# Softmax reciprocals spread by two small DMAs through DRAM, one bias tile per graph, and the waits in another order

## The reference, cut to what matters

```
h = max(layernorm(x), 0); x = x + cheb(h, adj)           # Chebyshev propagation, 4 orders
h = max(layernorm(x), 0); x = x + attention_net(h, adj)  # tanh encoder, 2 masked attention layers, 3-layer MLP
h = max(layernorm(x), 0); x = x + relu(norm_adj @ (h @ W))
h = max(layernorm(x), 0); t = adj @ h; x = x + where(t > 0.5, t / t, 0)

def att_layer(h, mask):                                  # inside attention_net, twice per graph
    v, q, k = tanh(h @ wv + bv), tanh(h @ wq + bq), tanh(h @ wk + bk)
    att = softmax(q @ k.T * mask - 9e15 * (1 - mask), axis=2)
    return att @ v
```

## Time and profile before

| | |
|---|---|
| median of 3 runs | 888.2 us (886.36 to 890.27) |
| profiled execution, its own time | 887.01 us |
| its span (first to last instruction) | 885.2 us |
| PE busy | 768.6 us, 87% of the span |
| DVE busy | 576.3 us, 65% |
| ACT busy | 445.8 us, 50% |
| POOL busy | 388.1 us, 44% |
| DMA | 22.77 MB, 26 GB/s over the span |

### The profile page before, as it was taken

How to read it: one execution, slowest core, us unless ns; L and a number is a source line. 1 busy time by engine, 2 the same in 40 slices (tenths; PEclk the granted TensorE clock), 3 DMA queues, 4 the chain that set the end, 5 groups by cost and what they waited for, 6 DMA issues and landing times.

```text
span 885.2 us, 11494 instructions
## 1 busy us (share of the span) xinstructions
PE 768.6 (87%) x3776; PEld 541.5 (61%) x3808; DVE 576.3 (65%) x1631; ACT 445.8 (50%) x929; POOL 388.1 (44%) x491
## 2 busy tenths in 40 slices
PE   2658799999989899999989999998989999998774
PEld 2435566666766666666766666675766666675543
DVE  3266668577677767677677767667676767765432
ACT  2035645637364654737464553736464563735330
POOL 3134534555353535555353435546263445543301
PEclk9969999999999999999999999999999999999996
DMA  6100100102010100201010100102010010000000
GB/s 168 39 1 0 54 1 5 56 1 59 1 60 1 57 4 0 60 1 60 1 61 1 30 31 0 60 1 61 1 60 0 14 47 1 7 1 7 1 7 6
DMA packets 29276, 22.77 MB, mean 26 GB/s; under 512 B 19488, under 2 KB 21024, under 8 KB 29216
## 3 DMA queue, kind: packets, MB, share of 16 engines
q1 hardware_dynamic: 29216, 22.03, 8.3%
HBM read 19.93 MB, written 2.10 MB: 25 GB/s over the span
## 4 chain that ended last, share of the span: by engine, by line
PE 38%; DVE 22%; POOL 18%; issue 17%; ACT 4%; POOLq 0%; DVEq 0%
PE turn_ps L1056 7%; PE pre_ps L936 5%; PE post_ps L936 4%; POOL rstd_pre L414 4%; DVE u L831 3%; PE turn_ps L1039 3%; POOL rstd_post L414 3%; POOL k_lo L486 2%; DVE h_nat_pre L706 2%; PE pre_ps L899 2%; PE pre_ps L953 2%; POOL centred_pre L417 2%; POOL centred_post L417 2%; DVE score_ps L795 2%; DVE negz L803 2%
## 5 line engine op out<-in xcount | busy, mean ns | idle before, releaser
L589 ACT ACTIVATE negz<-negz,negmax 128x512 f32<-128x512 f32 x128 | 92.3, 721 | 72.0 <-DVE negmax L803 72.0
L414 POOL TENSOR_TENSOR rstd_post<-vareps_post,nhalf 128x4 f32<-128x4 f32 x32 | 32.8, 1026 | 210.1 <-DVE vareps_post L691 210.1
L1056 PE MATMUL turn_ps<-pt,v_n 128*128 128x512 f32 x256 | 115.2, 592 | 0.0
L803 DVE CUSTOM_DVE_ANT_0 negz<-score_ps,gate 128x512 f32<-128x512 f32 x128 | 88.5, 692 | 19.7 <-DVE score_ps L795 6.2
L795 DVE TENSOR_TENSOR score_ps<-score_ps,a_nat 128x512 f32<-128x512 f32 x128 | 89.1, 696 | 17.1 <-PE score_ps L1025 16.1
L936 PE MATMUL pre_ps<-at_hi,u_pair_pre 128*128 128x512 f32 x192 | 87.6, 456 | 7.3 <-DVE u_pair_pre L728 5.2
L414 POOL TENSOR_TENSOR rstd_pre<-vareps_pre,nhalf 128x4 f32<-128x4 f32 x32 | 34.0, 1061 | 131.1 <-DVE vareps_pre L691 131.1
L548 ACT ACTIVATE y_t_pre<-pre_ps 128x512 f32<-128x512 f32 x48 | 28.7, 597 | 123.3 <-PE pre_ps L936 123.3
L596 ACT ACTIVATE pt<-turn_ps 128x512 f32<-128x512 f32 x128 | 74.0, 593 | 15.8 <-PE turn_ps L1039 13.9
L936 PE MATMUL post_ps<-at_hi,u_pair_post 128*128 128x512 f32 x128 | 55.7, 435 | 29.5 <-DVE u_pair_post L728 29.5
L1039 PEld LDWEIGHTS turn_ps<-ident,negz 128*128 128x128 f32 x512 | 61.2, 141 | 32.3 <-issue 16.1
(11 more groups left out here) (137 smaller groups left out, 1815.4 us busy)
## 6 DMA issues: line engine op xcount, KB each, us to landing
a_nat<-in_adj SPq DMA_DIRECT2D x16, 1024.0 KB, 5.8
x_in<-in_x SPq DMA_DIRECT2D x16, 128.0 KB, 2.8
out<-x_out SPq DMA_DIRECT2D x16, 128.0 KB, 1.9
cheb_ws<-in_L_gnn_weight SPq DMA_DIRECT2D x2, 64.0 KB, 4.7
att_w<-in_L_gnn_a_wv SPq DMA_DIRECT2D x2, 64.0 KB, 2.4
att_w<-in_L_gnn_a_wk SPq DMA_DIRECT2D x2, 64.0 KB, 2.2
att_w<-in_L_gnn_a_wq SPq DMA_DIRECT2D x2, 64.0 KB, 2.2
bv_f<-in_L_gnn_a_bv SPq DMA_DIRECT2D x2, 64.0 KB, 2.7
```

The costliest lines, as they stand in the source:

```text
L414: gp.tensor_tensor(rstd[t][:], vareps[t][:], nhalf[:, 0:RB], ALU.pow)\
L589: sc.activation(probs[:, i, :], negz[:, i, :], ACT.Exp, bias=negmax[:, i:i + 1], scale=-1.0, accum_out=total[:, i:i + 1]).then_inc(probs_d ...
L803: ve.tensor_tensor_reduce(negz[:, i, :], score_ps[i % 2][:], gate[:, i, :], -1.0, 3.0e38, ALU.add, ALU.min, negmax[:, i:i + 1]).then_inc(b ...
L1056: mm = te.matmul(turn_ps[0][:], v_n[a][:, j * P:(j + 1) * P], pt[:, j, :], start=(j == 0), stop=(j == RB - 1))
```

## The change

Three edits go together.

1. `spread_inv` on PE and `copy_inv` on ACT are gone. In their place SP issues two DMAs for each attention layer (`spread`): the 128 x 4 reciprocals to a 2 KB tensor in DRAM, `inv_d`, and, when that has landed, from there to all 128 partitions of `inv_row`. They come from DRAM in the order partition, then block, so DVE reads `inv_row` with a step of four elements (16 bytes).
2. `gate` is made once per graph, at the place of the first attention layer.
3. Where an instruction has several waits, their order in the source is turned in nine places, so that the one that comes last in time is written first.

```diff
 "tensor":  ... keys.1-1 turn_a1-0 [spread_inv.2-2 taken out] values.1-1 turn_a2-0 turn_a3-0 attend.2-2 ...
 "scalar":  copy_inv.2-2 and copy_inv.1-1 taken out
 "gpsimd": """
-        norm_cheb-0 add_cheb_bias-0 split_qk.1-1 mask_bias.1-1 inverse_roots-0 cheb_u3-0
-        norm_gcn-2 mask_bias.2-1 split_qk.2-1 cheb_f0-0 norm_last-2 norm_enc-0
+        norm_cheb-0 add_cheb_bias-0 split_qk.1-1 mask_bias-1 inverse_roots-0 cheb_u3-0
+        norm_gcn-2 split_qk.2-1 cheb_f0-0 norm_last-2 norm_enc-0
...
+        inv_d = nc.dram_tensor("inv_d", [P, RB], F32)
...
+            def spread(g, a):
+                sp.wait_ge(inv_done, 2 * g.n + a + 1)
+                if follows(g, a):
+                    sp.wait_ge(inv_spread, 16 * (2 * g.n + a))
+                sp.dma_start(inv_d[:], inv_total[:]).then_inc(inv_sent, 16)
+                sp.wait_ge(inv_sent, 16 * (2 * g.n + a + 1))
+                if follows(g, a):
+                    sp.wait_ge(attended, 2 * g.n + a)
+                sp.dma_start(inv_row[:], inv_d.rearrange("p i -> (p i)").partition_broadcast(P))\
+                    .then_inc(inv_spread, 16)
...
-            load(Graph(0, 3))
-            store(Graph(0, 0))
-            for n in range(1, B):
+            spread(Graph(0, 0), 0)
+            for n in range(B):
+                if n:
+                    store(Graph(0, n - 1))
+                spread(Graph(0, n), 1)
                 if n + SLOTS < B:
                     load(Graph(0, n + SLOTS))
-                store(Graph(0, n))
+                if n + 1 < B:
+                    spread(Graph(0, n + 1), 0)
+            store(Graph(0, B - 1))
...
@@ mask_rows (DVE)
-                if i == 0:
-                    dve.wait_ge(gate_done, 2 * g.n + a + 1)
+                dve.wait_ge(masked, 8 * g.n + n + 1)
+                if n == 0:
+                    dve.wait_ge(gate_done, g.n + 1)
                 if follows(g, a):
                     dve.wait_ge(pt_ready, 8 * g.n + n - 3)
-                dve.wait_ge(masked, 8 * g.n + n + 1)
@@ invert (DVE)
                 dve.wait_ge(probs_done, 8 * g.n + 4 * a + 4)
+                if follows(g, a):
+                    dve.wait_ge(inv_sent, 16 * (2 * g.n + a))
@@ attend (DVE)
-                dve.wait_ge(inv_copied, 2 * g.n + a + 1)
                 dve.wait_ge(pv_ready, 2 * g.n + a + 1)
-                ve.tensor_tensor(to[:], turn_ps[0][:], inv_row[:], ALU.mult).then_inc(attended, 1)
+                dve.wait_ge(inv_spread, 16 * (2 * g.n + a + 1))
+                ve.tensor_tensor(to[:].rearrange("h (i p) -> h i p", p=P),
+                                 turn_ps[0][:].rearrange("h (i p) -> h i p", p=P),
+                                 inv_row[:].rearrange("h (p i) -> h i p", i=RB),
+                                 ALU.mult).then_inc(attended, 1)
```

More of the change, by code:

```diff
@@ L471, in cheb_f0, with mask_bias @@
                 pool_pre.add(gp.tensor_tensor(c_diff[:], c_diff[:], over_blocks(d_root[:]), ALU.mult))
+                pool.wait_ge(pool_pre.sem, pool_pre.so_far())
                 pool.wait_ge(cheb_taken, 3 * g.n + 3)
-                pool.wait_ge(pool_pre.sem, pool_pre.so_far())
                 gp.tensor_tensor(f0[:], f0[:], c_diff[:], ALU.add).then_inc(f0_done, 1)
-            def mask_bias(g, a):
-                if follows(g, a):
-                    pool.wait_ge(biased, 8 * g.n + 4 * a)
+            def mask_bias(g):
+                if follows(g):
+                    pool.wait_ge(biased, 8 * g.n)
                 gp.tensor_scalar(gate[:], a_nat[g.slot][:], -1.0, NEG, ALU.add, ALU.mult)\
@@ L507, in _ @@
                 "add_mlp_bias": add_mlp_bias,
-                **layer(0, split_qk=queries_keys, mask_bias=mask_bias),
+                "mask_bias": mask_bias,
+                **layer(0, split_qk=queries_keys),
                 **layer(1, split_qk=queries_keys),
-                **layer(1, mask_bias=mask_bias),
                 "norm_gcn": scale_norm("post", 0), "norm_last": scale_norm("post", 1),
@@ L599, in copy_pt @@
                 return f
-            def copy_inv(g, a):
-                act.wait_ge(inv_ready, 2 * g.n + a + 1)
-                sc.activation(inv_row[:], turn_ps[1][:], ACT.Copy).then_inc(inv_copied, 1)
             def mlp(k, to, ps, bias):
@@ L696, in norm_apply @@
                 dve.wait_ge(rstd_done[t], 4 * g.n + 2 * k + 2)
+                if t == "pre" and k == 0 and follows(g):
+                    dve.wait_ge(ht_ready, 2 * g.n)
                 to = h_nat[t][:, :, 0, :] if t == "pre" else h_nat[t][:]
@@ L735, in cheb_norm @@
             def cheb_norm(g):
-                if follows(g):
-                    dve.wait_ge(ht_ready, 2 * g.n)
                 norm_apply("pre", dve_pre, g, 0)
@@ L1041, in turn_rows, with attend @@
                 mm.then_inc(pt_ready, 1)
-            def spread_inv(g, a):
-                pe.wait_ge(inv_done, 2 * g.n + a + 1)
+            def attend(g, a):
                 pe.wait_ge(pt_copied, 8 * g.n + 4 * a + 4)
-                for i in range(RB):
-                    mm = te.transpose(turn_ps[1][:, i * P:(i + 1) * P],
-                                      inv_total[:, i:i + 1].to_broadcast([P, P]), ident[:])
-                mm.then_inc(inv_ready, 1)
-            def attend(g, a):
                 pe.wait_ge(qkv_done, 10 * g.n + 5 * a + 5)
-                pe.wait_ge(pt_copied, 8 * g.n + 4 * a + 4)
                 for j in range(RB):
```

28 lines of the change are left out of this document (14 added, 14 removed).

## The result

The changed kernel takes 873.36 us, median of 4 runs (871.59 to 874.47), beside 888.42 (886.36 to 890.27) for the kernel before in the same comparison: ratio 0.9829, 95% interval 0.9802 to 0.9856. Forecast were 870 us and a range of 864 to 881. The profiled execution took 871.59 us with a span of 869.7, so 15.5 us of span are gone; the prediction's sum had 18.5.

A forecast was written before the change was run, and what follows sets the result against it. The lead was taken to alternate between PE and the DVE/POOL chain. 14 x (0.45 + 0.44 + 0.36) = 17.5 us, with rounds 1 and 16 18.5 off 887.0: 868.5; the median lies 1.2 higher, so 870 us, range 864 to 881.

The forecast's parts named there:

- the stepped read: DVE's scaling reading inv_row: forecast 0; rival 0.53 us in each of 15 rounds (second layer), about 877 us, chance 0.28.
- second bias tile: POOL's tile slows DVE's `u` before the third layer's propagation; without it PE's idle time goes, 0.45 us a round.
- first layer's transposes: Four PE transposes before the first layer's product: 0.44 us a round with the tile gone, nothing alone.
- waits: Late wait carried by the operation, at masks and first-layer scaling: 0.36 us a round (0.13, 0.05 and 0.18).
- The two DMAs: Reciprocal to `inv_row`: 2.2 plus 3.2 us and 0.1 for wake-ups, 5.5 us, bounds 4.6 and 9.2; hidden in full rounds.
- The product's 0.8 us to spare: First layer: transfers land at 430.5, PE's product is there at 431.3, so the transfers have 0.8 us to spare.
- The point from which lateness costs: First layer's scaling, ahead of PE's queries: from 7.2 us of transfers on, each us more costs one.
- The rival: Late transfers hold the first layer's scaling and PE's queries: slower than before, about 898 us at the bad end, chance 0.07.
- The last round: Only PE's product of 3.6 us hides the transfers there; their cost put at what the transposes gave: nothing.

The follow-up runs named there:

- e1: The kernel before with the bias tile made once per graph and nothing else: 877.48 us, ratio 0.9882.
- e3: The kernel before with the waits in the new order and nothing else: 880.7 us, ratio 0.9921.
- e9: The changed kernel plus one ScalarE copy per layer that takes the step out of the reciprocals, so DVE reads contiguous columns: 872.75 us, ratio 0.9835.
- e2: The kernel before with the reciprocals spread by the two DMAs and nothing else: 896.17 us, ratio 1.0097.
- e6: The kernel before with the bias tile once per graph and the new wait order, reciprocals still spread by PE: 870.67 us, ratio 0.9817; repeated 871.43 us.
- e4: The changed kernel with reciprocals written to DRAM as 512 pieces of 4 bytes, so inv_row is read without a step: 1141.16 us, ratio 1.2856.
- e7: The changed kernel with one more 2 KB DRAM-to-DRAM transfer between the two DMAs: 886.75 us, ratio 0.9992.
- e10: The changed kernel plus ScalarE's copy that removes the step, but the last graph's second layer spread by PE as before: 867.73 us, ratio 0.978.
- e5: The changed kernel, with DVE's scaling multiplying by a constant tile read at steps 1, 2, 3, 4 or 8: one run, 874.01 us.

## Why the prediction was right, and where it was off

The time lay in the range, 3.4 us above the forecast, between the forecast's own bounds (up to 873) and those of its likeliest rival, the stepped read (about 877; by its own terms 878). Round for round:

| step of the prediction | forecast, us a round | measured |
|---|---|---|
| second bias tile | -0.45 | -0.64 (e1: -0.68) |
| first layer's transposes, once the tile is gone | -0.44 | -0.39 |
| waits | -0.36 | -0.44 (e3) |
| stepped read, second layer | 0 | +0.31 (against e9; e2: +0.35) |
| sum | -1.25 | -1.15 (the parts: -1.16) |

That the sum of a round is so close is partly luck: the gains of the tile and the waits were put 0.27 us too low, the cost of the stepped read 0.31 too low, and the two errors nearly cancel. The mechanisms, where each edit acts and what it waits on, are what was right.

**The bias tile**: right in its mechanism (`u` at 0.42 us, no idling before the propagation), mis-sized by reading the printed 0.45 us of idle time as the whole of the wait.

**The transposes**: worth nothing alone and their own time with the tile gone. Both halves were shown: e2 turns them into idle time, and e9, whose scaling has no step, is 0.39 us a round below e6, where PE still makes them. The forecast's 0.44 are read from the start of the product in the round of the earlier trace rows:

```profile
428.13 3.60 PE L1056 MATMUL turn_ps<-pt,v_n 128*128 128x512 f32 x8
```

The three parts alone sum to -0.68 - 0.44 + 0.35 = -0.77 us a round, together they give -1.15; the 0.38 more is this term. 0.05 of the 0.44 is missing: from the product's start to the start of PE's next work it is 3.03 us before, 3.08 after.

**The waits**: by e3, the front gave 0.13, for which 0.18 were forecast (0.05 of them for the scaling); the stretch with the second layer's masks gave 0.29 instead of 0.18. That is the worth of some three of its four masks, at 0.10 each; I had counted fewer, because DVE idles there.

**The two DMAs**: 5.5 us forecast, 5.4 measured, from parts that were each wrong: the write lands in 1.4 us (2.2 assumed), the broadcast in 4.0 (3.2 assumed). The Trainium skill's rule for pieces under 512 bytes ("DMA: Bandwidth & Descriptors", Specifications), weighed as speaking against this write, costs nothing to be seen at 16 bytes, for the write lands sooner than any other transfer of the trace; e4 shows a price at 4 bytes. The Trainium skill's "Anatomy of one DMA" on the same page was weighed there too, but it describes transfers that GpSimd issues; here SP issues them, and the write's 1.4 us are less than the 2.0 that it gives as the fixed part. The product's 0.8 us to spare are there: in the round shown above the broadcast is issued at 417.64 and lands 4.0 us later, at 421.6, and the product releases the scaling at 422.56. The point from which lateness costs was put at 7.2 us after the reciprocal's end for a scaling of 0.69 us, or 7.4 after its start; less the 0.38 by which the scaling grew that is 7.0, and e7 shows 7.05. The rival was rightly placed, each us past the point costs one as it said, and it didn't come because in the full rounds the transfers were in time.

**The stepped read**: this is the step that failed as a choice. I took 0 because the nearest row was a contiguous one; the rival had 0.53 us in each of 15 rounds, 8 us. Measured, the scaling is 0.38 us longer, and 0.31 of it pass on, 4.7 us in 15 rounds: the next operation starts 1.00 us after the scaling's start (406.08 to 407.08), 0.69 after it in e6 and e9. The place was right: the second layer's scaling sits on the chain and pays, the first layer's has room.

**The last round**: put at nothing, it cost 2.75 us against the kernel before. From reciprocal to scaling it is 6.94 us in the second layer where PE's way took 5.62, and 6.29 in the first; the two scalings are 0.38 longer each. The 2.75 are what is left after a gain, since the bias tile and the waits are worth something in this round too, which the prediction had not counted: e6, which has them and lets PE spread, is 2.2 us shorter there than the kernel before. Against e6 the two DMAs cost 4.9 us: 0.73 and 1.39 from reciprocal to scaling, 0.76 in the two scalings, if all of it passes on, and the remaining 2.0 come with a lower granted clock (0.96 against 1.00 up to the last scaling, 0.70 against 0.75 from there on). e10 shows how much of it hangs on the last graph's second layer: 5.3 us less than e9 in these two stretches, 73.1 against 78.4. It still needs 4.4 us more there than e6, with 7.69 us from reciprocal to scaling in the last graph's first layer, which goes by the transfers, against 5.56; to leave that layer to PE too was not tried. How PE's wait and the clock hang together stays open (see the table at e10).

## What to carry to other kernels

Moving work from the engine that leads to a DMA gives that engine's time only while another engine still has work to cover the round trip; count the last pass by itself, and consider leaving the old way there, as e10 does for the last layer. When a DMA brings data in an inconvenient order, price both ways to undo it before choosing: here the step of 16 bytes costs 0.38 us at each read, the strided write of 4-byte pieces 7.3 us at each transfer, and a copy of 1.12 us on ScalarE, which idles there, all but nothing in a full round. And ask each part of a compound change what it does alone: two of the three carried all of the gain here.

## What was not expected of the hardware

- A DMA of 2 KB into DRAM lands in 1.4 us as 128 pieces of 16 bytes and in 8.7 us as 512 pieces of 4 bytes.
- DVE reads float32 with a step of 2 at full speed; 512 columns take 0.69, 0.69, 0.84, 1.07 and 1.14 us at steps 1, 2, 3, 4 and 8 (e5; one operand in PSUM, without a step).
- The wait that an instruction carries itself should be the late one: the mask's two operations are 0.87 us apart with three waits in the old order, 0.73 in the new one (e3).
- After waits of 3.7 us in the last round TensorE went on at the lower clock for 10 us (e9, e7). After shorter and longer ones the granted clock of these 10 us was between 0.67 and 1.00, not in the order of the waits: one and the same program had 0.81 and 1.00.
- What DVE lost beside POOL has moved, not gone: `c` (L783) now takes 1.53 us beside POOL's `q_lo`, where it took 1.26 before. It starts as much earlier behind PE's last fold (1.59 us instead of 1.86), so nothing comes of it.
